# First stage of a token, attention and expert kernel rebuilt: order of the steps, split products, normalizations on ScalarE, joined table rows, and GpSimd's power behind its DMAs

## The reference, cut to what matters

```python
h = concat([token_table[x], concat([op, var, const, struct, special])[x]], -1)   # two tables, 128 channels each
a = layernorm(h)
q, k, v = split(a @ W_qkv + b_qkv)             # 16 heads of 16
pq, pk = elu(q) + 1, elu(k) + 1
h = h + pq @ (pk^T v) / (pq . sum(pk) + 1e-6)  # linear attention within a row of 128 tokens
x2 = layernorm(h)
logits = l2norm(x2) @ l2norm(sim_matrix) - sigmoid(gates)      # 16 experts
mask = (logits > 0), or the top two where none is
rw = softmax over mask of relu(logits)
q, k, v = sum_e rw[e] * (x2 @ proj[e])         # three projections of 256 x 128 for each expert
ao = causal softmax attention of q, k, v
out = h + sum_e rw[e] * (ao @ o_proj[e])
```

## Time and profile before

| what | value |
|---|---|
| median of three runs | 1186.64 us |
| the profiled execution, its own time | 1176.88 us |
| its span, first to last instruction | 1175.0 us |
| TensorE busy, mean granted clock | 88%, 0.973 of full |
| VectorE, ScalarE, GpSimd busy | 79%, 45%, 64% |
| DMA, over the span | 143.28 MB, 122 GB/s |

### The profile page before, as it was taken

One profiled execution on the slowest core, in us unless ns is written; L12 is line 12 of the kernel. 1 busy time (PEld: TensorE's weight loads), 2 busy tenths in 40 slices (PEclk: granted clock), 3 DMA queues, 4 the chain that ended last, 5 costly groups with the idle time before them and its releaser, 6 DMA issues.

```text
span 1175.0 us, 26735 instructions
## 1 busy us (share of the span) xinstructions
PE 1029.2 (88%) x6571; PEld 862.2 (73%) x6572; DVE 928.9 (79%) x3134; ACT 533.6 (45%) x1455; POOL 754.4 (64%) x975
## 2 busy tenths in 40 slices
PE   1999999999999993599999959999999999999898
PEld 0565656565666662588988849999999889988897
DVE  3789999999999996245544528999888888888898
ACT  3544444444433431234443425555555555555554
POOL 6657777777777756700000037888888888888785
PEclk9999999999999995799999979999999999999999
DMA  5642333333222225576777752333333333333230
GB/s 141 201 151 88 100 104 99 104 95 100 77 86 86 80 75 197 180 231 221 239 223 232 224 177 77 95 91 91 90 90 89 89 89 89 89 89 89 85 93 32
DMA packets 108096, 143.28 MB, mean 122 GB/s; under 512 B 15388, under 2 KB 95330, under 8 KB 107876
## 3 DMA queue, kind: packets, MB, share of 16 engines
q1 hardware_dynamic: 88004, 91.17, 24.4%
q0 software_dynamic: 18880, 50.36, 15.0%
q10 hardware_dynamic: 1152, 1.05, 0.3%
HBM read 77.37 MB, written 72.46 MB: 128 GB/s over the span
## 4 chain that ended last, share of the span: by engine, by line
PE 40%; DVE 22%; POOL 18%; issue 13%; ACT 3%; DMA 2%; POOLq 1%; SPq 0%; DVEq 0%; ACTq 0%
PE bank L1366 8%; PE bank L1291 7%; PE bank L1293 7%; PE bank L1292 7%; PE bank L1298 5%; POOL row_y L747 5%; POOL qk_neg L732 2%; POOL x2T L732 2%; PE bank L1364 2%; DVE phi L1055 2%; POOL x2T L728 2%; POOL x2T L734 2%; POOL qk_neg L728 2%; DVE h L1075 1%; POOL sorted_x L674 1%
## 5 line engine op out<-in xcount | busy, mean ns | idle before, releaser
L1291 PE MATMUL bank<-wo_hi,split_lo 128*128 128x256 f32 x1024 | 302.8, 296 | 4.6 <-DVE qk_e L1228 2.2
L1292 PE MATMUL bank<-wo_lo,split_hi 128*128 128x256 f32 x1024 | 287.3, 281 | 0.0
L1293 PE MATMUL bank<-wo_hi,split_hi 128*128 128x256 f32 x1024 | 287.2, 280 | 0.0
L1291 PEld LDWEIGHTS bank<-wo_hi,split_lo 128*128 128x128 f32 x1024 | 194.5, 190 | 9.3 <-DVE qk_e L1228 4.6
L1366 PE MATMUL bank<-w_attn,x1T 128*128 128x512 f32 (+1 forms) x512 | 201.2, 516 | 0.0
L1292 PEld LDWEIGHTS bank<-wo_lo,split_hi 128*128 128x128 f32 x1024 | 194.5, 190 | 0.0
L1293 PEld LDWEIGHTS bank<-wo_hi,split_hi 128*128 128x128 f32 x1024 | 194.0, 189 | 0.0
L843 ACT ACTIVATE h<-bank,rwo 128x256 f32<-128x256 f32 x256 | 107.4, 471 | 126.8 <-PE bank L1293 99.5
L747 POOL DMA_INDIRECT row_y<-sorted_y,pair_now x128 | 128.4, 1003 | 36.3 <-issue 28.5
L1166 DVE TENSOR_TENSOR split_lo<-bank,split_hi 128x256 fp32r<-128x256 f32 x144 | 61.2, 425 | 104.2 <-ACT split_hi L812 103.0
L740 POOL COPY pair_now<-pair_at 128x2 uint32 (+1 forms) x64 | 13.1, 205 | 195.7 <-SPq L531 195.6
(11 more groups left out here) (223 smaller groups left out, 2516.0 us busy)
## 6 DMA issues: line engine op xcount, KB each, us to landing
sorted_y<-row_y SPq DMA_DIRECT2D x36, 384.0 KB, 3.1
sorted_y<-w_attn SPq DMA_DIRECT2D x36, 384.0 KB, 3.2
row_x<-sorted_x SPq DMA_DIRECT2D x72, 128.0 KB, 2.4
h_rows<-h SPq DMA_DIRECT2D x64, 128.0 KB, 1.8
row_x<-h_rows SPq DMA_DIRECT2D x64, 128.0 KB, 2.9
out_h<-row_x SPq DMA_DIRECT2D x64, 128.0 KB, 2.0
category_table<-in_L_tok_special_table SPq DMA_DIRECT2D x10, 623.0 KB, 5.0
phi<-sorted_x SPq DMA_DIRECT2D x36, 128.0 KB, 2.1
```

What stands on the lines that cost most here:

```text
L1291: pe.matmul(ps, left[1][c], right[0][c], start=(c == 0), stop=False)
L1292: pe.matmul(ps, left[0][c], right[1][c], start=False, stop=False)
L1293: last = pe.matmul(ps, left[0][c], right[0][c], start=False, stop=(c == n - 1))
```

## The change

1. **Products.** `W_qkv` and the turned x1 are split into a high and a low float32r part (in buffers that stage 2 and 3 use later). Each attention product is the bias and six float32r products (low x high, high x low, high x high, two halves of the channels) instead of the bias and two float32 products. ScalarE's copy of x1T makes the high part; a new VectorE instruction, `x1_lo`, the low one.
2. **Normalizations.** x1 and x2 move from VectorE to ScalarE (scale and bias for each row). VectorE computes the bias of both in a new small instruction `centers` at the start of its step, behind the power. The reciprocal at L1089 goes; the norm of x2 is multiplied together for each group (`energy`, two small instructions).
3. **Gate.** Only top values, top indices, counts and places stay in stage 1. The weights of the two experts are worked out once for all tiles at the start of stage 2, and the full table `routing` in five instructions of 1024 elements in its steps 0 to 4. Groups are of four tiles up to tile 55, then of two.
4. **Joined rows.** SyncE copies both tables, in ten steps, side by side into `embed_table` (rows of 512 B at a distance of 1 KB), so that from tile 14 on one gather brings a tile. The first 14 tiles still take three.
5. **Later weights.** Two parts of q, k, v in each of the steps -7 to -1, then one in each step to 33; the 16 parts of `o_proj` are loaded and split in steps -8 to 7 of stage 2.
6. **Orders.** All four engines get another order of the pieces. On GpSimd a step is now gathers, scatters, power. Scatters of a tile come in step t+6, for the groups of two in step (first tile)+4. The ring of x2 has 9 buffers instead of 11. Stage 1 ends with step 66.

```diff
-    N_X2, N_RAW = 11, 4
-    SCATTER_LAG = 7
+    GROUPS = [(t, QUAD) for t in range(0, B - 8, QUAD)] + [(t, 2) for t in range(B - 8, B, 2)]
+    N_X2, N_RAW = 9, 4
+    LAST_STEP = B + 2
...
+        def scatters_at(step):
+            tiles = []
+            for first, n in GROUPS:
+                at = first + n + 2
+                tiles += [t for t in range(first, first + n) if step == (at + t - first if n == QUAD else at)]
+            return tiles
...
         def weights_at(i):
             if -7 <= i < 0:
-                return range(4 * (i + 7), 4 * (i + 8))
-            n = 28 + i
-            return [n] if n < 4 * E else []
+                return range(2 * (i + 7), 2 * (i + 8))
+            n = 14 + i
+            return [n] if 14 <= n < 3 * E else []
...
# SyncE, stage 1
+                if 0 <= i.c - COPY_FROM < COPIES:
+                    for skip, at, src in ((N_SMALL, HALF, special_table), (0, 0, token_table)):
+                        n = -(-src.shape[0] // COPIES)
+                        lo, hi = n * (i.c - COPY_FROM), min(n * (i.c - COPY_FROM + 1), src.shape[0])
+                        sp.dma_start(embed[skip + lo:skip + hi, at:at + HALF], src[lo:hi, :]).then_inc(rows_joined, 16)
...
# GpSimd, stage 1 (the power at the end; it stood at the start)
+                elif gather.inside(B):
+                    if gather.c == JOINED_FROM:
+                        pool.wait_ge(rows_joined, 16 * (2 * COPIES + 4))
+                    pool.indirect_dma_start(out=h[gather.c % 8], out_offset=None, in_=embed,
+                                            in_offset=offsets(ids[:, gather.c, 0:1])
+                                            ).then_inc(rows_gathered[gather.q], 16)
+                for t in scatters_at(i.c):
+                    quad_done(pool, "position_index", group_of(t))
+                    for n in range(2):
+                        pool.indirect_dma_start(out=sorted_x, out_offset=offsets(position_u[:, t, n:n + 1]),
+                                                in_=x2[t % N_X2], in_offset=None
+                                                ).then_inc(scattered[t % N_X2], 16)
                 row = i.c + 4
                 if 0 <= row < N_ROOTS:
                     pool.wait_ge(done["roots_in"], row + 1)
                     pool.tensor_tensor(roots[:, row, :], roots_in[:, row, :], minus_half[:, 0:3], ALU.pow
                                        ).then_inc(done["roots"], 1)
...
# ScalarE, stage 1, behind the exponential
+                    after(act, "centers", tile)
+                    act.activation(x1[:, :], h[t % 8], ACT.Identity, scale=roots[:, t, 0:1],
+                                   bias=centers[:, t, 0:1]).then_inc(done["x1_normed"], 1)
...
+                    scatter_done(act, t - N_X2)
+                    after(act, "centers", tile.shift(3))
+                    act.activation(x2[t % N_X2], h2[tile.p][:, :], ACT.Identity, scale=roots[:, t + 3, 1:2],
+                                   bias=centers[:, t + 3, 1:2]).then_inc(done["x2_normed"], 1)
...
# VectorE, stage 1, start of a step
+                row = i.c + 4
+                if 0 <= row < N_ROOTS:
+                    dve.wait_ge(done["roots"], row + 1)
+                    dve.scalar_tensor_tensor(centers[:, row, :], moments[:, row, :, 0], -1.0, roots[:, row, 0:2],
+                                             ALU.mult, ALU.mult).then_inc(done["centers"], 1)
...
# its order then: phi, den, statistics of tile i+6, zden, x1_lo, attn, h2, its statistics, roots_in, and
+                for back, piece in ((2, rows_placed), (1, rows_counted), (0, experts_chosen)):
+                    g = group_at(i.c - back)
+                    if g is not None:
+                        piece(g)
# then the first moments, kvm, and the low half of a weight
...
# TensorE
+            def attn_product(tile, ps, lo, hi, name):
+                pe.matmul(ps[:, 0:hi - lo], ones_r[0:BIAS_ROWS, :], bias[:, lo:hi], start=True, stop=False)
+                for c in range(CH):
+                    for x, w, end in ((1, 0, False), (0, 1, False), (0, 0, c == CH - 1)):
+                        last = pe.matmul(ps[:, 0:hi - lo], turned[x][c], w_attn_s[w][:, c, lo:hi], start=False,
+                                         stop=end)
# its order then: rank, attn_sums, turn x1, logits, turn phi, turn x2, qk product, kv product, v product
```

More of the change, by code:

```diff
@@ L775, in step1 @@
                     after(act, "qk_negative", tile)
+                    after(act, "phi", tile.shift(-1))
                     act.activation(qk_e[:, :], qk_neg[:, :], ACT.Exp, scale=-1.0).then_inc(done["qk_exp"], 1)
@@ L950, in rows_counted @@
             def rows_counted(g):
-                dve.tensor_scalar(active[:, :, :], logits[:, :, :], 0.0, None, ALU.is_gt)
-                dve.tensor_scalar(idle[:, :], top[:, :, 0], 0.0, None, ALU.is_le)
+                first, n = GROUPS[g]
+                tiles = slice(first, first + n)
                 gate_wait("top_indices")
-                numbers = over_quad(expert_no)
-                dve.tensor_tensor(is_one[:, :, :], numbers, top_at[:, :, 0:1].broadcast_to([P, QUAD, E]),
+                quad_done(dve, "rank_product", g - 1)
@@ L1326, in step1 @@
                 if tile.inside(B):
-                    after(pe, "x1_T", tile.shift(-1))
+                    after(pe, "x1_lo", tile.shift(-1))
                     after(pe, "x1_normed", tile)
                     turn(ps_x1, *halves(x1)).then_inc(done["x1_turned"], 1)
+                if i.inside(B):
+                    g = group_of(i.c)
+                    t = i.c - GROUPS[g][0]
+                    if t == 0:
+                        quad_done(pe, "gate_scaled", g - 1)
+                    after(pe, "x2_T", i)
+                    if i.c == 0:
+                        pe.wait_ge(setup_v, 7)
+                    for c in range(CH):
+                        last = pe.matmul(ps_logits[g % 2][:, t, :], halves(x2T)[c], simn[:, c, :],
+                                         start=(c == 0), stop=(c == CH - 1))
+                    last.then_inc(done["logits_product"], 1)
+                tile = i.shift(3)
+                if tile.inside(B):
+                    after(pe, "phi_q_T", tile.shift(-1))
+                    after(pe, "phi", tile)
+                    turn(ps_pq, *halves(phi)).then_inc(done["phi_q_turned"], 1)
                 tile = i.shift(1)
@@ L1334, in step1 @@
                     turn(ps_x2, *halves(x2[tile.c % N_X2])).then_inc(done["x2_turned"], 1)
+                tile = i.shift(4)
+                if tile.inside(B):
+                    after(pe, "phi", tile.shift(-1))
+                    after(pe, "x1_lo", tile)
+                    if tile.c == 0:
+                        pe.wait_ge(setup_v, 6)
+                    attn_product(tile, ps_qk, 0, 2 * C, "qk_product")
                 tile = i.shift(3)
@@ L1337, in step1 @@
                     after(pe, "v_copied", tile)
-                    after(pe, "phi_q_T", tile.shift(-1))
                     after(pe, "kv_masked", tile.shift(-1))
-                    after(pe, "phi", tile)
-                    turn(ps_pq, *halves(phi)).then_inc(done["phi_q_turned"], 1)
                     for g in range(G):
```

510 lines of the change are left out of this document (273 added, 237 removed).

## The result

The changed kernel takes **1262.81 us** (median of 4 runs, 1258.19 to 1266.24) against 1186.26 beside it: a ratio of 1.064 [1.061, 1.068], slower by 77 us. The profiled execution has a span of 1259.6 us (before 1175.0). The forecast was 1210 with a range to 1245: the direction is right, the time lies outside.

A forecast was written before the change was run, and what follows sets the result against it. VectorE's queue was taken to set the pace, 6.50 us a step. Rows 10 to 64 -4, start +18, seam +6 and stage 2 +3.5 sum to +23.5, on 1186.64 us 1210; the 8-in-10 range was 1168 to 1245.

The forecast's parts named there:

- The hold, wait (c): Stage 1, GpSimd: power queued behind two scatters makes VectorE stand 2.65 us once in four steps, 36 us in all.
- TensorE's clock in the hold: Rival, stage 1: TensorE loses its clock in each GpSimd hold, 1.7 us times 14 groups, +23, 1233; chance 0.15.
- The steps without hold: Stage 1, rows 10 to 64: VectorE's work 21.8 us per four steps plus waits; hold included, 346 against 351, -4.
- the waits for kv: Stage 1, step without a gate piece: kv stands behind the qk product, 0.75 us once in four steps, 10 in all.
- those ahead of `x1_lo`: Stage 1: VectorE waits for x1's high part, 0.22 us in each step, bounds 0 and 0.4, 12 in all.
- TensorE's term: Stage 1: TensorE's work falls from some 5.7 to 4.7 us a step, which alone brings nothing but buys slack.
- Start, +18: Up to row 10: table copies in 512 B rows at 50 ns delay the weights, 107 against 88.5, +18 us.
- the lower end at which -7 was forecast: Start: with 27 ns for each 512 B row the compute sets the pace, -7 us.
- Seam, +6: Row 64's root inputs to stage 2's first turn: scatters wait for positions ahead of the power, 48 against 41.7, +6.
- Stage 2, +3.5, and 3, 0: Stage 2: o_proj parts split ahead of the first pair 2.5, five large instructions 1, +3.5; stage 3 keeps its queues, 0.
- Faster: Rival: ScalarE hands x1 over in time, kv is never late, copies run at large-copy rate; -18, 1169; chance 0.22.
- Few engines: Rival, start: copy row counts that 16 does not divide leave engines idle; +33 to +36 at the start, 1226; chance 0.18.

The follow-up runs named there:

- TensorE filled: Changed kernel with 15 more products of 384 columns on TensorE in the first step of each group of four: 1227.53 us, ratio 1.033.
- power first: Changed kernel with GpSimd's power ahead of gathers and scatters: 1203.42 us, ratio 1.013.
- power between: Changed kernel with GpSimd's order gathers, power, scatters: 1182.41 us, ratio 1.001.
- power between, two gathers: power between with joined rows undone, special table copied whole, two gathers a tile from tile 14: 1178.62 us, 0.998; repeated on another chip 1180.13, 1.000.
- the runs with early loads: First four o_proj loads ahead of the zero fills, on power between, two gathers: 1193.86 us (with 8 copy pieces 1191.45); on power between: 1180.49 us.

## Why the prediction failed, point by point

| profile | row 10 | rows 10 to 64 | seam | to the end | mean clock, 110 to 440 us |
|---|---|---|---|---|---|
| changed kernel | 107.4 | 402.4 | 49.7 | 700.2 | 0.88 |
| TensorE filled | 108.8 | 366.7 | 49.9 | 700.8 | 0.99 |
| power first | 120.9 | 337.1 | 43.3 | 698.7 | 0.97 |
| power between | 103.9 | 334.2 | 43.0 | 702.8 | 0.98 |
| power between, two gathers | 90.3 | 342.7 | 43.2 | 700.9 | 0.99 |

- **The hold, wait (c): right in mechanism and size.** Forecast 36 us in the 54 steps; with the clock kept it is 366.7 - 334.2 = 32.5, and the first group's hold, ahead of row 10, adds 3.4. Its place was right to the instruction.
- **TensorE's clock in the hold: the step that failed.** It was set down as a rival with a chance of 0.15 and 1.7 us in each of 14 groups, 23 us, and left out of the sum. The runs show it there and worth 35.7 us, 2.7 in each of the 13 groups, against 1.7: not only the qk product runs at half rate but everything of the 6 us behind the hold, the turns and the logits too, and the wait of `kvm`, forecast as 0.75, is 2.92 where it is 0.68 with the clock kept. The argument for a low chance was that stage 1 had 1.00 before; but the forecast itself put 3 us holes into it, and in the earlier trace rows the clock fell behind 3 us in which TensorE was half busy.
- **The steps without hold: mis-sized by 24 us.** 346 less the hold's 36 is 310 us; the run with the power between has 334.2. VectorE's timeline there gives the terms. Four steps with a weight (187.31 to 212.12 us, from `centers` to `centers`) take 24.8 us, forecast 23.4 without the hold: the waits for kv are 0.76 (0.75 forecast, right), those ahead of `x1_lo` 1.82 (0.88 forecast), VectorE's work 22.2 (21.8). Four without a weight (301.35 to 324.82) take 23.5, forecast 22.5: 0.75 for kv, 0.42 ahead of `x1_lo`, 0.89 for the exponential and the sums, which were in no term, and 21.4 of work (20.8). That makes some 16 of the 24 us; the other 8 lie in the groups in which the clock fell for 3 to 4 us (from 221, 273 and 392 us on) and in the first one. TensorE's term was "some 4.7 us a step"; it is 5.53 (the earlier trace rows price only the products), so it has no slack where VectorE has no gate piece. The six products of 512 take 1.50 (1.4 forecast), those of 256 0.83 (0.7); the rest, two biases, kv, sums, logits and three pairs of turns, was put at 2.6 and takes 3.0, and 0.18 is idle. ScalarE's x1 takes 0.60 us, not the 0.45 drawn from the earlier trace rows, by the groups of ScalarE, 120 to 440 us, each shape apart (busy us, mean ns):

```profile
L844 ACT ACTIVATE x<-h,centers,roots 128x256 f32<-128x256 f32 x20 | 12.0, 601 | 25.1 <-DVE centers L1095 24.3 <-issue 0.8
```

- **Start, +18: the right sum by a wrong price, and so by luck.** 50 ns a packet were taken, the row says 28.7, next to the lower end at which -7 was forecast; the DMA share was 0.67 from 16 to 100 us, not near 1. What the rows show is late weights, not a full DMA: behind the copies SyncE needs 3 to 4 us for most issues of a load of 128 KB, with two gathers mostly 0.58. With the power between, ScalarE waits for weights for 13.5 us of q_proj and k_proj from 40 to 107 us, and with two gathers no such wait reaches 2.6 us; the joined rows are worth 13.6 us at the start, the power behind the gathers and scatters 3.4 (107.4 - 103.9). TensorE's clock goes along here too, 0.92 from 16 to 100 us and 1.00 with two gathers; its part of the 13.6 was not isolated. SyncE's timeline, the changed kernel's and that with two gathers, then ScalarE's waits with the power between:

```profile
76.66 3.38 SPq L500 DMA_DIRECT2D raw<-in_L_ffn_k_proj  x1
```
```profile
70.90 0.58 SPq L499 DMA_DIRECT2D raw<-in_L_ffn_v_proj  x1
```
```profile
ACT wq_hi L505 <- DMA raw<-in_L_ffn_k_proj: 6.9, 3, 3.9
ACT wq_hi L505 <- DMA raw<-in_L_ffn_q_proj: 6.6, 3, 3.9
```

  "Min transfer for line-rate" of the Trainium skill (DMA: Bandwidth & Descriptors, Specifications) was nearer to this price than the row that the forecast preferred: 512 bytes in 28.7 ns are 17.8 GB/s an engine, against 19 in the whole copy. It did not give the start its time all the same.
- **Seam, +6: right**, +8.0. Two holds of four scatters each, 5 us of GpSimd's waiting for positions in both; with the power ahead of the scatters the seam is 43.0 to 43.3, so 6.7 of the 8 are the order.
- **Stage 2, +3.5, and 3, 0:** +6.0 together. The 5.1 us at the first pairs were under-priced (2.5), and the runs with early loads take 2.5 and 5.6 us of the stretch back.
- **The rivals.** "Faster" needed holds and waits nearly absent. By its own numbers its stage 1 was wrong, too: four steps at 24.5 and 23.5 us make 324, which is -27 and not -20 (the power between took 334.2). "Few engines" is worth 5 us at the start, not 15 to 18; its +33 to +36 follow from 62 ns alone, and the 52 it names first give +21, 3 above the forecast. No single rival was the answer, because the forecast treated the clock as an alternative to its own sum where it was a consequence of it: hold 36 and clock 36 come together, but for the two falls without a hold. In spans the sum closes: 23.5 forecast, 35.7 for the clock, 24 for the steps, -3.5 for the hold, and 5.5 for start, seam and stages 2 and 3 are 85, and 1259.6 - 1175.0 is 84.6. The medians lie 77 apart, since the profiled execution of before was 9.4 us below the median beside the changed kernel and that of the changed kernel 1.4 below its own.

So the order of GpSimd's queue costs 32.5 + 35.7 + 6.7 + 3.4 = 78.3 us, against 75.7 between the spans of the changed kernel and the power between (1259.6 and 1183.9), whose last stretch is 2.6 us longer; of the rest, 16.4 us are gained in the steady steps and 15.4 lost at the start, and by the medians nothing is left. No version was found that beats the kernel before by more than 0.2%.

## What to carry to other kernels

An in-order queue that serves two consumers should have the instruction that the fastest loop waits for ahead of any whose input is made later in the same round, and behind those whose result the same loop needs next: here gather, power, scatter gave 1.001 of the time before, power first 1.013 and power last 1.064. When a forecast puts a hole of some microseconds into a full TensorE, its clock belongs into the sum and not among the rivals: here it about doubled the price of the hole. An instruction costs nothing where its queue would wait, and its full time where it would not: the same statistics cost nothing ahead of `x1_lo` and 24 us behind the root inputs. And when work leaves the engine that sets the pace, add up the next two engines row by row before promising its gain, since a gain ends at the first of them.

## What was not expected of the hardware

- A hole of 3 us in TensorE's work once in some 30 us was enough for 4 to 10 us at 0.50 of the clock each time (6 of them from 409 to 415 us), and filling 2.9 us of it with products that nobody reads kept 1.00 in both windows shown and gave 35 us.
- A queue nearly all of whose packets were of 512 bytes, written from HBM to HBM at a stride of 1 KB, took 28.7 ns a packet with 71.6% of the engines' time taken, less than the 38 ns of the earlier trace rows for loads and stores of a quieter stretch, so here a packet's time from a quiet stretch did not carry over to a busy one. Behind such copies most issues of a load of 128 KB took SyncE 3 to 4 us, without them mostly 0.58.
- The start was slower by 13.5 us when its gathers stood behind an operation of 0.88 us, through rows that landed 6 us after their issue.
